# Attention scores that run six heads behind the maxima in place of seven, with the picks of q spread over twelve half steps

## What is computed

```python
q = x @ Wq.T; k = x @ Wk.T; v = x @ Wv.T
qh = q.reshape(b, s, N_QUERY, N_HEAD, D_HEAD)        # 4 x 8 heads of width 16
kh = k.reshape(b, s, N_HEAD, D_HEAD)
scores = jnp.einsum('bsqhd,bthd->bqhst', qh, kh) * scale
probs = jax.nn.softmax(scores, axis=-1)
a_dot = jnp.einsum('bqhst,bthd->bsqhd', probs, vh)
a_mem = sigma_q @ memory / (sigma_q @ memory_norm)
out = a_dot * (1.0 - w) + a_mem * w
```

## Time and profile before

| | |
|---|---|
| median of 3 runs | 5969.57 us (5966.69 to 5977.84) |
| the profiled execution | 5961.26 us, its span 5959.4 us |
| mean granted clock of PE | 0.912 of full |
| busy: PE, DVE, ACT, POOL | 86%, 60%, 42%, 12% of the span |
| first reduction of a batch to that of the next | 221 to 223 us, 16 batches |
| first to last reduction of the maxima in a batch | 105.7 to 105.9 us |

### The profile page before, as it was taken

How to read it: one execution, slowest core, us unless ns; L and a number is a source line. 1 busy time by engine, 2 the same in 40 slices (tenths; PEclk the granted TensorE clock), 3 DMA queues, 4 the chain that set the end, 5 groups by cost and what they waited for, 6 DMA issues and landing times.

```text
span 5959.4 us, 156553 instructions
## 1 busy us (share of the span) xinstructions
PE 5125.7 (86%) x62928; PEld 3669.1 (62%) x62928; DVE 3602.6 (60%) x7842; ACT 2488.3 (42%) x4659; POOL 696.8 (12%) x917
## 2 busy tenths in 40 slices
PE   4888888888888885789889889889889889889888
PEld 3777777777777774555655655555555555555555
DVE  3565556655555663656656656656656656656656
ACT  2333333333333331446445445445445445445535
POOL 0000000000000000111111111111111111111121
PEclk8889998998889996899999999999999999999999
DMA  1222222222222221000000000000000000000000
GB/s 57 56 63 53 53 53 53 59 62 62 53 53 53 53 59 53 26 15 1 16 15 1 16 15 1 16 15 1 16 15 1 16 15 1 16 15 3 14 15 8
DMA packets 352735, 173.84 MB, mean 29 GB/s; under 512 B 300032, under 2 KB 300800, under 8 KB 351264
## 3 DMA queue, kind: packets, MB, share of 16 engines
q1 hardware_dynamic: 343056, 146.25, 9.5%
q10 hardware_dynamic: 8976, 17.30, 1.0%
HBM read 94.79 MB, written 67.63 MB: 27 GB/s over the span
## 4 chain that ended last, share of the span: by engine, by line
issue 29%; PE 20%; DVE 7%; POOL 3%; ACT 1%; DMA 0%; DVEq 0%; POOLq 0%; SPq 0%; ACTq 0%
PE row_psum L40 5%; PE row_psum L42 5%; PE row_psum L41 5%; DVE smax L1755 2%; POOL xs L1211 2%; PE row_psum L1477 1%; PE row_psum L1340 1%; DVE stats L1581 1%; PE row_psum L1444 1%; PE row_psum L1445 1%; POOL rstd L1183 1%; PE row_psum L1459 1%; DVE xr_lo L1610 1%; DVE xs L1684 0%; DVE probs L1592 0%
## 5 line engine op out<-in xcount | busy, mean ns | idle before, releaser
L1755 DVE TENSOR_REDUCE smax<-row_psum 128x1 f32<-128x512 f32 x2048 | 1282.0, 682 | 316.5 <-PE row_psum L1477 315.4
L1309 ACT ACTIVATE probs<-row_psum 128x512 f32<-128x512 f32 x2048 | 1113.3, 602 | 508.2 <-PE row_psum L1490 403.9
L1477 PE MATMUL row_psum<-k_stack,q_stack 128*128 128x512 f32 x2048 | 881.3, 442 | 28.1 <-DVE smax L1755 24.4
L1490 PE MATMUL row_psum<-q_stack,k_stack 128*128 128x512 f32 x2048 | 842.5, 425 | 22.1 <-ACT probs L1309 13.8
L1477 PEld LDWEIGHTS row_psum<-k_stack,q_stack 128*128 128x128 f32 x2048 | 400.7, 196 | 461.6 <-DVE smax L1755 384.7
L1502 PE MATMUL row_psum<-probs,v_aug 128*32 128x512 f32 x4096 | 538.9, 604 | 9.2 <-ACT av_sb L1322 9.2
L1490 PEld LDWEIGHTS row_psum<-q_stack,k_stack 128*128 128x128 f32 x2048 | 384.3, 193 | 251.9 <-ACT probs L1309 194.7
L40 PE MATMUL row_psum<-wf_hi,xr_hi 128*128 128x320 f32 (+1 forms) x1024 | 327.7, 320 | 13.9 <-DVE xr_lo L1610 13.3
L860 DVE TENSOR_TENSOR lane_t<-lane_t,lane_p 128x30 f32<-128x30 f32 (+14 forms) x960 | 318.5, 332 | 33.0
L857 DVE TENSOR_TENSOR lane_p<-lane_t 128x30 f32<-128x30 f32 (+14 forms) x960 | 316.0, 329 | 24.5
L1340 PE MATMUL row_psum<-ident,probs 128*128 128x128 f32 x784 | 173.9, 378 | 176.1 <-DVE probs L1592 176.1
(11 more groups left out here) (207 smaller groups left out, 10262.2 us busy)
## 6 DMA issues: line engine op xcount, KB each, us to landing
xs<-x SPq DMA_DIRECT2D x17, 1024.0 KB, 5.6
x_sp<-in_x ACTq DMA_DIRECT2D x33, 512.0 KB, 4.2
tri_dram<-tri SPq DMA_DIRECT2D x256, 64.0 KB, 3.3
lane_t<-tri_dram SPq DMA_DIRECT2D x32, 512.0 KB, 4.0
inv_dram<-lane_t SPq DMA_DIRECT2D x32, 512.0 KB, 2.6
inv_b<-inv_dram SPq DMA_DIRECT2D x256, 64.0 KB, 2.4
x_res<-in_x SPq DMA_DIRECT2D x32, 512.0 KB, 3.4
x<-x_res SPq DMA_DIRECT2D x32, 512.0 KB, 4.8
```

The costliest lines, as they stand in the source:

```text
L1309: act.activation(probs[:, h % PROBS, tt, :], ps[:, m % STACK_BANKS, :], ACT.Exp, scale=float(DH) ** -0.5).then_inc(exp_ready, 1)
L1477: pe.matmul(ps[:, STACK_BANKS + m % MAX_BANKS, :], q_stack[:, qt, P * st:P * st + P], k_stack[:, kv, :], start=True, stop=True).then_inc(m ...
L1490: pe.matmul(ps[:, m % STACK_BANKS, :], k_stack[:, kv, P * tt:P * tt + P], q_stack[:, qt, :], start=True, stop=True).then_inc(score_mm, 1)
L1755: dve.tensor_reduce(smax[:, g, st:st + 1], ps[:, STACK_BANKS + (NT * g + st) % MAX_BANKS, :], AX.X, ALU.max).then_inc(max_ready, 1)
```

## The change

SCORE_LAG goes from 7 to 6, and with it AV_LAG from 8 to 7, TURN_LAG from 12 to 11 and OUT_LAG from 13 to 12. The attention loop has 44 steps in place of 45. Since the picks of q have to be done before the first score, the 15 that lie in the loop now go into 12 half steps in place of 14: `picks` gives 2, 1, 1, 2, 1, 1, 1, 2, 1, 1, 2 and 0 of them.

```diff
-SCORE_LAG = 7
+SCORE_LAG = 6
@@
+        def picks(half_step):
+
+            first = lambda k: min(NQ * HP, 2 + (NQ * HP - 2) * k // (2 * SCORE_LAG - 1)) if k else 1
+            return range(first(half_step), first(half_step + 1))
+
@@ ACT
-                            first = 1 + 2 * g + j
-                            if g < SCORE_LAG and first > 2:
-                                q_pair(first)
-                                if first == 2 * SCORE_LAG:
-                                    q_pair(first + 1)
+                            if g < SCORE_LAG:
+                                for m in picks(2 * g + j):
+                                    if m > 2:
+                                        q_pair(m)
@@ PE
-                            first = 1 + 2 * g + j
                             if g < SCORE_LAG:
-                                pick_q(first)
-                                if first == 2 * SCORE_LAG:
-                                    pick_q(first + 1)
+                                for m in picks(2 * g + j):
+                                    pick_q(m)
```

## The result

| | before | changed |
|---|---|---|
| median of 6 runs | 5977.09 us (5966.69 to 5983.41) | 6127.74 us (6099.52 to 6142.81) |
| ratio to before, 95% interval | | 1.0258 (1.0242 to 1.0273) |
| the profiled execution, its span | 5961.26, 5959.4 us | 6127.39, 6125.5 us |
| PE busy, mean granted clock | 86%, 0.912 | 83%, 0.911 |

A forecast was written before the change was run, and what follows sets the result against it. PE's queue sets the steady pace, and the cut lag exposes the DMA chain of the maxima: 2.6 + 7.0 - 0.4 - 0.8 = 8.4 us a batch, 16 batches +134, so 6100 us. Own range 6070 to 6150; stated range 6050 to 6200; chance 0.63.

The forecast's parts named there:

- Landing 7.13 us after the turn, unchanged by the lag: Steady quad: the last of four DMAs putting maxima into `q_stack` lands 7.13 us after PE turns the maxima, as before.
- PE comes to the score after 5.64: Steady quad: with four pairs and one values step fewer, PE reaches the waiting score 5.64 us after the turn, not 8.69.
- Landing to start, 0.2 us: Quad's first score starts 0.2 us after the last DMA lands, so 7.33 us after the turn.
- Score to next turn, 7.80 less 0.3 for waits that go: Steady quad: 7.5 us from first score to next turn, giving period 14.83 against 13.44; five such periods cost +7.0 a batch.
- Quad 1, +2.6: From the turn of quad 1 to that of quad 2, each batch takes 2.6 us longer.
- Quad 7, -0.4: Last quad of a batch: its first score starts at 4351.5 against 4351.90, so 0.4 us sooner.
- emptier queue of ACT in the tail, -0.8: From quad 7's first score to the end: same work, but ACT's queue starts empty, so 0.8 us of waits go.
- Picks and front, 0, with bounds from 0 to +2.1: Front of a batch: earlier picks cost 0 to 1.4 us, quad 0's DMA wait up to 0.7; both taken as 0.
- Sum, +8.4 a batch: Per batch 2.6 + 7.0 - 0.4 - 0.8 = 8.4 us, over 16 batches +134 us.
- rival B: New stalls also drop PE's clock to 1.2 GHz: half of seven stalls gives +90 us, 6190; all gives 6280; chance 0.20.
- Signs: Expected in the trace: 1.5 us PE gap, 14.8 us period, busy share 0.9, front within 1 us, tail over 1 us shorter.
- Rival D: Faster: landing 5.6 us after the turn, no stall, 1.7 us a batch gained, 5943 us; chance 0.04.

The follow-up runs named there:

- without the wait: Changed kernel, lag 6, with the four DMAs writing pieces to an unread tile, PE waiting only at the quad's last score, maxima not subtracted: 5913.59 us, ratio 0.9899.
- the stalls filled: Changed kernel, with PE issuing six or nine matmuls nobody reads ahead of the wait for the DMAs in quads 1 to 7: 6075.72 us, ratio 1.0175.
- the picks alone: Kernel before, SCORE_LAG still 7, with only the changed kernel's `picks` over the first twelve half steps: 5952.13 us, ratio 0.9964.
- The copy ahead of the exponentials: Changed kernel, lag 6 and new picks, with ACT's copy to `shift` put ahead of its half step's two exponentials: 5936.16 us, ratio 0.9931.
- with a shorter chain: Changed kernel with ACT's copy ahead of the exponentials and two DMAs of two rows in place of four of one: 5909.77 us, ratio 0.9873.
- with two DMAs: Changed kernel, ACT's copy where it was, with two DMAs of two rows in place of four of one row: 5927.22 us, ratio 0.9912.

## Why the prediction was right, point by point

The prediction said 6100 us and slower; it is 6128, inside its range. Its steps:

- *Landing 7.13 us after the turn, unchanged by the lag.* 7.13 in the row shown, 7.12 to 7.15 as the medians of quads 2 to 5. Right. In quad 6 the median is 7.43: in half of the batches the last DMA takes 2 us or more there. Why was not looked into.
- *PE comes to the score after 5.64.* The changed kernel hides this; without the wait it is 5.60. Right, so the count of pairs and values steps in PE's order was a sound way to get it.
- *Landing to start, 0.2 us.* 0.09 by the row (4174.66 to 4174.75), with a landing known to a tenth; over all quads that waited, the trace has 0.04 to 0.05. The 0.2 was a misreading: the score of the earlier trace rows started 8.67 us after its turn and had waited for nothing, so 0.2 was the slack that was left.
- *Score to next turn, 7.80 less 0.3 for waits that go.* 7.59 (4174.75 to 4182.34), so 0.2 goes. Period 14.81 in the row, 14.77 as the median, against 14.83. The five periods cost 7.65 us in the mean, forecast 7.0: the late landings of quads 2 and 6 and the clock make the rest (with the stalls filled it is 6.67).
- *Quad 1, +2.6.* +3.2. It goes with the clock, batch by batch: 13.1 us where PE stays at 2.4 GHz (3 batches); 13.3 to 14.1 with a stretch at 1.2 GHz near the turn, where every batch had one before (5); 14.5 with one behind the new stall (6); 15.6 and 16.2 with one in both places, or a longer one behind the stall (2). The forecast, 13.6, took the old stretch along and no new one. With the stalls filled the mean is 13.46, 2.5 more than before.
- *Quad 7, -0.4; emptier queue of ACT in the tail, -0.8.* -0.5, and 0.0. The tails at full clock are 0.9 shorter (16.76 against 17.67), so the mechanism was there, and the low clock behind the 2.2 us gap of quad 7, in ten batches of 16, ate it. This term failed.
- *Picks and front, 0, with bounds from 0 to +2.1.* -1.2 in the mean, outside the bounds. This term failed too. The bounds allowed for costs alone. The low stretch at the start of every batch was in the trace of before, and the 0.92 of the front in the earlier trace rows pointed to it; I had not looked at it by its clock. The bound of +0.7 for the new wait of quad 0 holds: the front is 0.4 longer than with the picks alone in the changed kernel, 0.7 with the stalls filled.
- *Sum, +8.4 a batch.* +9.0. It is the lag with its stalls 8.7 (forecast 8.4), clock +2.1 (forecast 0, as rival B), picks -1.8 (forecast 0). The two terms that I had left out almost cancel. The main one was worked out right, and that the total is so close is luck. The forecast's own range was also added up a little low at the top: 24 and 34 us above 6100 are 6158, not 6150.
- *Signs.* The gap of 1.4, the period of 14.8, the busy share of 0.9 (13.37 of 14.81) and the 10 us from first to last maximum (10.5) came out. The front changed by 1.2 and not by under 1, and from the turn of quad 7 to the end it is 0.5 shorter and not a little over 1.

Rival B was partly true. Its full form is not: the typical gap of 1.4 us was not followed by 1.2 GHz once, and of the 80 steady quads 7 had such a stretch. Its price of 90 us was too high in both factors. It put a stretch behind half of seven stalls a batch; there were 26 behind 128 stalls. And it counted half of each as lost: 6.1 us less at 1.2 GHz, from 30.0 to 23.9, gave back 2.1, a third. That PE is not what everything waits for in those stretches would explain this; it was not tried. Rival D put the lag without its stall at -1.7 us a batch and the kernel at 5943. The lag without its stall is worth -2.7. The copy ahead of the exponentials, which the prediction named as what D needs, gave 5936, but 1.8 us a batch of that are the picks'; the lag's part is 220.04 - 218.76 = 1.3, since quads 0, 1 and 7 still wait.

## What to carry to other kernels

A lag between a producer and its consumer is worth its slack: before it is cut, list the chain that it covers (here 7.13 us, of which 1.8 are issues spaced at 0.6 and 2.3 a place in ACT's queue) and set it against the time at which the consumer will now come. If it comes too early, shorten the chain first, and then cut the lag; the same change was worth +2.6% or, with a shorter chain, -1.3% (0.4 of that from the picks). And put into the sum what idle time does to the clock of PE, in both directions.

## What was not expected of the hardware

- PE's clock after short gaps. In the changed kernel the gap ahead of a quad's first score was under 1.9 us in 88 cases, and no stretch at 1.2 GHz stood at any of them; of the 40 longer ones (up to 3.2 us) 26 had one, begun in the gap or at most 1.6 us behind it. It is not a sharp limit: with two DMAs, 2 of 8 gaps between 1.3 and 1.9 us had one. Before, one stood at the start of every batch, behind gaps of 1.41 and 0.22 us; with the 1.41 alone, in the picks-only kernel, none did. The Trainium skill, "TensorE: Matmul & The Clock Gate", section "HAM oscillation — how this bites in real kernels", tells of exposed waits for DMAs that are longer than the bursts of work between them, each followed by the low clock. Here gaps of a sixth of a quad did it in some quads and not in others. The typical wait here, 1.4 us in a quad with 13.4 us of work, is not that loop, so the prediction stretched the section when it made rival B, in its full form, the forecast by it.
- Matmuls that compute nothing, put into a stall that stays, made the kernel 50 us faster.
- A DMA of two rows from SP takes 0.5 us to issue, as one of one row (0.6) or half a row (0.6): the number of DMAs sets it, not the bytes.
- Landings of these small DMAs take 1.7 us in the median and up to 3.5. The late ones are few, but where the slack is gone each costs its whole lateness, and in the three latest of the changed kernel (gaps of 2.3, 2.7 and 3.2 us in quad 2) the clock fell with it.
